# A fused attention kernel: queries, late weights and row sums reordered in its start

## The reference

```
# first block, per image (1024 pixels, 256 channels)
x_ln = layernorm(x);  q = x_ln @ wq + bq
o    = gelu(depthwise_conv7x7_stride2(q as an image) + dw_b)     # 16 x 16 positions
pos  = refs + tanh(o @ pw_w)                                     # 256 sampling points
samp = bilinear(x, pos)                                          # from x itself
k, v = samp @ wv + bv, then @ mk_w, @ mv_w;  qh = q @ mq_w
att  = softmax(qh kh^T) vh                                       # 8 heads, 1024 x 256
z    = att @ mo + mo_b + x;  y = gelu(layernorm(z) @ mlp_w + mlp_b) + z
# second block, per image
theta, phi, g = y @ w_theta, maxpool(y @ w_phi), maxpool(y @ w_g)
out  = y + sigma * (softmax(theta phi^T) g @ w_o + b_o)
```

## Time and profile before

| | us |
|---|---|
| three runs, median (lowest to highest) | 514.73 (513.17 to 515.65) |
| the profiled execution, its time | 512.36 |
| its span, first to last instruction | 510.6 |
| PE, DVE, ACT, POOL busy over the span | 454.9, 286.2, 211.6, 120.1 |
| mean granted clock of PE | 0.98 |

### The profile page before, as it was taken

How to read it: one execution, slowest core, us unless ns; L and a number is a source line. 1 busy time by engine, 2 the same in 40 slices (tenths; PEclk the granted TensorE clock), 3 DMA queues, 4 the chain that set the end, 5 groups by cost and what they waited for, 6 DMA issues and landing times.

```text
span 510.6 us, 9319 instructions
## 1 busy us (share of the span) xinstructions
PE 454.9 (89%) x3743; PEld 318.8 (62%) x3743; DVE 286.2 (56%) x609; ACT 211.6 (41%) x338; POOL 120.1 (24%) x163
## 2 busy tenths in 40 slices
PE   6788979988989999989899999989899897888956
PEld 5657756645567576656686666656767564665735
DVE  4518446846673367667754345567546647625433
ACT  1122212545346045655333336745173664662230
POOL 5420301167003001681002003761030030100000
PEclk9999989989999999999999999999999998999978
DMA  7298866581947930293157801472226200000202
GB/s 211 76 168 171 163 101 126 85 169 65 137 69 99 233 54 3 85 124 64 42 101 103 164 3 46 90 111 27 83 42 86 83 3 2 1 2 2 82 2 83
DMA packets 30489, 42.90 MB, mean 84 GB/s; under 512 B 6075, under 2 KB 21230, under 8 KB 30446
## 3 DMA queue, kind: packets, MB, share of 16 engines
q1 hardware_dynamic: 23598, 34.82, 37.4%
q0 software_dynamic: 3584, 4.50, 3.8%
q10 hardware_dynamic: 3264, 2.99, 2.9%
HBM read 16.16 MB, written 4.19 MB: 40 GB/s over the span
## 4 chain that ended last, share of the span: by engine, by line
PE 57%; DVE 13%; DMA 10%; POOL 7%; issue 5%; ACT 5%; SPq 1%; ACTq 0%; DVEq 0%; POOLq 0%
PE ps_d L759 8%; PE ps_d L884 5%; PE ps_d L861 5%; PE ps_d L961 5%; PE ps_d L747 4%; PE ps_s L808 4%; DMA xa<-in_x_dram 4%; PE ps_v L850 4%; DMA corners<-in_x_dram,row_of 3%; PE ps_v L844 3%; PE ps_t L827 3%; PE ps_d L779 3%; POOL samp L1937 3%; DVE mx L1613 3%; PE ps_d L903 2%
## 5 line engine op out<-in xcount | busy, mean ns | idle before, releaser
L1226 ACT ACTIVATE prob<-ps_t 128x1024 f32<-128x1024 f32 x64 | 65.4, 1021 | 95.8 <-PE ps_t L827 92.2
L1613 DVE TENSOR_REDUCE mx<-ps_s 128x4 f32<-128x1024 f32 x64 | 78.2, 1222 | 24.1 <-PE ps_s L808 23.2
L1909 POOL DMA_DIRECT2D q_st<-mx_t x64 | 34.0, 532 | 244.0 <-ACT mx_t L1218 226.0
L759 PE MATMUL ps_d<-cstack,conv_w 128*32 128x256 f32 x1024 | 59.0, 380 | 3.4 <-issue 1.8
L808 PE MATMUL ps_s<-k_st,q_st 96*128 96x256 f32 x256 | 49.9, 317 | 8.2 <-DVE mx L1613 7.1
L759 PEld LDWEIGHTS ps_d<-cstack,conv_w 128*32 128x32 f32 x1024 | 36.3, 108 | 23.9 <-issue 6.2
L808 PEld LDWEIGHTS ps_s<-k_st,q_st 96*128 96x128 f32 x256 | 35.9, 191 | 20.5 <-DVE mx L1613 12.6
L827 PE MATMUL ps_t<-q_st,k_st 98*128 98x256 f32 x256 | 42.6, 289 | 6.2 <-ACT zt L1285 3.0
L827 PEld LDWEIGHTS ps_t<-q_st,k_st 98*128 98x128 f32 x256 | 35.5, 192 | 8.9 <-issue 5.1
L1627 DVE TENSOR_TENSOR att<-ps_v,rden 128x256 f32<-128x256 f32 x32 | 13.6, 424 | 43.2 <-ACT rden L1237 43.2
L844 PE MATMUL ps_v<-prob,vh 128*32 128x256 f32 x512 | 35.1, 392 | 1.5 <-DVE att L1627 1.5
(11 more groups left out here) (178 smaller groups left out, 744.7 us busy)
## 6 DMA issues: line engine op xcount, KB each, us to landing
q_st<-q_parts SPq DMA_DIRECT2D x42, 256.0 KB, 5.6
xa<-in_x_dram SPq DMA_DIRECT2D x8, 512.0 KB, 9.6
z_all<-in_x_dram SPq DMA_DIRECT2D x8, 512.0 KB, 7.9
out_dram<-z_all SPq DMA_DIRECT2D x8, 512.0 KB, 2.6
cstack<-qpad SPq DMA_DIRECT2D x22, 180.5 KB, 5.7
k_st<-cstack SPq DMA_DIRECT2D x22, 128.0 KB, 4.2
q_st<-z_all SPq DMA_DIRECT2D x6, 256.0 KB, 5.7
cstack<-att SPq DMA_DIRECT2D x6, 180.5 KB, 9.8
```

What stands on the lines that cost most here:

```text
L759: ins = pe.matmul(ps[32 * k:32 * k + 32, 0, :], conv_w[:, cb * 4 + k, y, x, :], cstack[:, cb, k, y:y + HG_, x:x + WG_], start=n == 0, stop ...
L1226: drain(act.activation(prob[:, u % 2, 2 * pr:2 * pr + 2].rearrange("p h m s -> p (h m) s"), ps_t[:], ACT.Exp), t_ring, "t", b, u, pr)
L1613: drain(dve.tensor_reduce(mx[:, u % 2, half, :], ps_s[:], AX.X, ALU.max), s_ring, "s", b, u, half)
```

## The change

On PE, ACT and DVE the second query group of the first half goes ahead of the convolution, and both groups of the second half ahead of the keys; the opening order of the PSUM tiles is rewritten to match. The first half of image 1's convolution does 8, 3 and 2 steps (before 6, 4 and 3) in the ramp and in slots (0, 0) and (0, 1). The loads of for_rest are cut in two: three of them (for_output) are issued in slot (0, 3) behind z of image 0, eight (for_second) in slot (1, 0); PE and DVE wait for each where it is first used. On ACT row_deviation(0, [1]) stands ahead of the copy of the turned wq. On DVE two of the four statistics of the second half stand behind row_shift of the first, and query_lo(0, 1, [0]) ahead of the second sampled.

```diff
-STEPS_OF_1 = range(6), range(6, 10), range(10, 13), range(13, TAPS * TAPS)
+STEPS_OF_1 = range(8), range(8, 11), range(11, 13), range(13, TAPS * TAPS)
...
-    order += [("qh", 0, 0, 0)] + [("conv", 0, cb) for cb in range(CB)] + [("off", 0), ("qh", 0, 0, 1)]
-    order += [("qimg", 1, 1, jp) for jp in range(2)] + [("qimg", 1, 0, 0), ("qh", 0, 1, 0), ("kh", 0)]
-    order += [("qh", 0, 1, 1), ("qimg", 1, 0, 1), ("conv", 1, conv_halves(1)[0])]
+    order += [("qh", 0, 0, hg) for hg in range(NHG)] + [("conv", 0, cb) for cb in range(CB)] + [("off", 0)]
+    order += [("qimg", 1, 1, jp) for jp in range(2)] + [("qimg", 1, 0, 0), ("qh", 0, 1, 0), ("qh", 0, 1, 1)]
+    order += [("kh", 0), ("qimg", 1, 0, 1), ("conv", 1, conv_halves(1)[0])]
...
 # SP, slots
+                if b == 1 and s == 0:
+                    for_second.start(sp)
...
                     if s == 3:
                         behind_max_row(b, 3)
                         load_z(b)
+                        for_output.start(sp)
...
 # SP, ramp
             stack_conv(0, 1)
+
+
             load_a(1)
-            for_rest.start(sp)
             stack_q(0, 0, [0])
...
 # PE, slots
                     project(m, 1, 1)
+                    if m == 0:
+                        for_second.wait(pe)
                     project1(m, "tp", w_tp, 0)
...
                 if s == 7 and b == 0:
-                    for_rest.wait(pe)
+                    for_output.wait(pe)
...
 # PE, ramp
-            queries(0, 0, [0])
+            queries(0, 0)
...
             offsets(0)
-            queries(0, 0, [1])
             q_image(1, 1)
             q_image(1, 0, [0])
             setup_values()
-            queries(0, 1, [0])
+            queries(0, 1)
             pe.wait_ge(setup_act, A_ALL)
             keys(0)
-            queries(0, 1, [1])
...
 # ACT, ramp
                 setup_copy(t_wqt, ps_s[:, 0:2, :])
-                row_deviation(0, [1])
...
             row_deviation(0, [0])
+            row_deviation(0, [1])
             setup_queries()
...
-            query_hi(0, 0, [0])
+            query_hi(0, 0)
...
-            query_hi(0, 0, [1])
             setup_values()
-            query_hi(0, 1, [0])
+            query_hi(0, 1)
...
-            query_hi(0, 1, [1])
...
 # DVE, slots
+                    if m == 0:
+                        for_second.wait(dve)
                     g_projected(m)
...
-                    for_rest.wait(dve)
+                    for_output.wait(dve)
...
 # DVE, ramp
-            half_stats(0, second)
+            half_stats(0, second[:2])
             row_shift(0, first)
+            half_stats(0, second[2:])
...
-            query_lo(0, 0, [0])
+            query_lo(0, 0)
...
             positions(0)
-            query_lo(0, 0, [1])
...
             sampled(0, 0)
+            query_lo(0, 1, [0])
             sampled(0, 1)
-            query_lo(0, 1, [0])
+            query_lo(0, 1, [1])
...
-            query_lo(0, 1, [1])
```

More of the change, by code:

```diff
@@ L424, in wait @@
                 eng.wait_ge(self.sem, 16 * len(self.pairs))
-        for_q, for_norm, for_image, for_conv, for_taps, for_fused, for_keys, for_rest = [
-            Loads(f"loaded_for_{name}") for name in ("q", "norm", "image", "conv", "taps", "fused", "keys", "rest")]
+        for_q, for_norm, for_image, for_conv, for_taps, for_fused, for_keys, for_output, for_second = [
+            Loads(f"loaded_for_{name}") for name in ("q", "norm", "image", "conv", "taps", "fused", "keys", "output", "second")]
         for_q.add(consts[:], a["shape_constants"][:, 0:K_M32])
@@ L450, in build @@
         for_keys.add_to_all_rows(mvb_all[:], a["L0_conv_mv_b"])
-        for_rest.add_matrix(mo[:], a["L0_conv_mo_w"])
-        for_rest.add_to_all_rows(mob_all[:], a["L0_conv_mo_b"])
-        for_rest.add_matrix(mlp[:], a["L0_conv_mlp_w"])
+        for_output.add_matrix(mo[:], a["L0_conv_mo_w"])
+        for_output.add_to_all_rows(mob_all[:], a["L0_conv_mo_b"])
+        for_output.add_matrix(mlp[:], a["L0_conv_mlp_w"])
         for_image.add_to_all_rows(mlpb_all, a["L0_conv_mlp_b"])
         for row in range(3):
[L456 to L461, removed]
+            for_second.add_matrix(w_tp[:, :, row * C8:(row + 1) * C8], a["L1_conv_w_theta"])
+        for_second.add_matrix(w_tp[:, :, 3 * C8:4 * C8], a["L1_conv_w_phi"])
+        for_second.add_matrix(w_g[:], a["L1_conv_w_g"])
+        for_second.add(w_o[:], a["L1_conv_w_o"])
+        for_second.add_to_all_rows(bo_all[:], a["L1_conv_b_o"])
+        for_second.add(sigma[:], a["L1_conv_sigma"].rearrange("(a c) -> a c", a=1).broadcast_to([P, 1]))
         def qpad_tile(b, cb):
```

## The result

The changed kernel is slower. Over 21 runs of each its median is 518.12 us (514.59 to 523.11) against 515.65 (509.75 to 518.55); the ratio is 1.0058, 95% interval 1.0037 to 1.0078. So it lost about 3 us where 6.95 were forecast as a gain, and lies outside the range of 505.0 to 511.8. They serve for places and mechanisms, the ratios for sizes.

A forecast was written before the change was run, and what follows sets the result against it. PE was busy 89%, but idle waits in the ramp before image 0's first scores were taken as what the change could shorten. -6.85 - 0.4 + 0.3 = -6.95 us, against median 514.73 giving 507.8; range 505.0 to 511.8.

The forecast's parts named there:

- Front, -3.2 and start of the convolution at 28.6: Image 0's second half of normalised rows comes 3.2 us earlier; its convolution starts at 28.6 instead of 31.49, -2.9.
- DVE's rows of image 1 and PE's convolution both move by 2.9, so the gather's first issue is at 48.5: Ramp: rows of image 1 move with the planes, to 38; gather's first issue moves from 51.45 to 48.5.
- The gather lands earlier after its issue: Ramp: with three query part DMAs gone, last landing 6.6 to 13.1 us after first issue, formerly 13.1; middle taken, 58.4.
- rival A: Gather lands no sooner after its issue, 13.1 us again, because planes alone keep the engines full: 511.6 us, chance 0.15.
- Six query part DMAs took 13.06 to issue against a full queue: SP's queue in the ramp: hence three such DMAs beside the gather are worth 6.5 us at most, nothing at least.
- New wait of DVE, keys at clock 1.00, gap of 1.6: DVE's query_lo ends 59.3, after the gather's landing; keys start 61.4 (-5.25) and, after PE's 1.6 gap, take 1.1 less.
- First scores at most 6.6 after key_hi: Ramp's end: key_hi, key_lo and key DMAs take at most 6.6 us, so first scores at 70.1 at latest.
- Loads in slots, +0.3: Loads moved to slot 3 of image 0 and the slot after: max rows may be late; +0.3 us taken.
- rival C: Loads of slot 3 hold max rows near 117, costing 6.3 us, the later eight again: 520.1 at full, chance 0.03.
- What arrives earlier there shifts all of the rest: After the first scores nothing is tied to a clock time, so a gain there reaches the end.
- -6.85 at the first scores: End of the ramp: first scores at 69.6 instead of 76.45 us, the largest term of the sum.
- Rival B: Ramp: planes start earlier and overlap key weights by up to 2.5 us; planes 2 late: 509.8 us, chance 0.14.

The follow-up runs named there:

- the front alone: Kernel before with only row_deviation of the second half ahead of the copy and two of four statistics behind row_shift; 0.9889 of before (0.9823 to 0.9955).

## Why the prediction was wrong

- *Front, -3.2 and start of the convolution at 28.6*: right. PE's second products at 17.28 (17.2 forecast), convolution at 28.32, ratio of the front alone 0.9889.
- *"DVE's rows of image 1 and PE's convolution both move by 2.9, so the gather's first issue is at 48.5"*: **this step failed**. It counted PE's two halves as one block that shifts, and the rows of image 1 as moving with the planes, to 38. The rows' second half landed at 39.5 and the gather was issued at 55.94. In the two kernels in which all or the eight small loads stood ahead of the copies, with the new order, the first issue came at 48.83 and 48.97: the step is right where the copies are not in the way. The loads were costed for who waits for them and for what lies beside the gather, not for what they had kept apart: six copies came right behind the rows and under the fetch of PE's own program. The row that would have warned is the 1.76 us gap for "issue" ahead of the second half, with DMA full; the prediction neither priced nor named it. Its cost is 8.9 us at the first scores, against the kernel with all loads back.
- *The gather lands earlier after its issue*: right in the changed kernel, and for another reason. Its four indirect DMAs landed in 3.9 us at the median from their issue, the last 9.1 after the first issue, and DVE's second blend did not wait for them. But there the planes of image 1 were issued only at 60.22, behind all four, because PE had made the q images late. In the four kernels in which the query copies were issued by 43 and the planes went out 2.6 us after the gather's first issue, the last corners landed 10.6 to 12.1 after it, against 13.1 before. So planes alone keep most of the landing time, as rival A said: the copies' absence is worth 1.0 to 2.5 us and not the middle of the range (3.2). Beside copies the landing was as bad as before or worse (up to 15.8).
- *"Six query part DMAs took 13.06 to issue against a full queue"*: misread, and the upper end of 6.5 rests on it. The three copies of the first group took 2.97 and those of the second 1.85; between them SP waited 8.2 us for DVE to make the second group's parts (who waits, for whom: total us, times, longest):

```profile
SPq L571 <- DVE q_parts L1530: 8.2, 1, 8.2
```

- *New wait of DVE, keys at clock 1.00, gap of 1.6*: right (gap 1.83, keys 1.97), shifted by the step that failed. It holds only as long as the gather lands in time: the gap was 1.8 to 2.9 in eight of the kernels with the new order, and 5.1 and 6.6 in the two whose last corners came 14 us or more after the first issue.
- *First scores at most 6.6 after key_hi*: missed by about 1. It was 7.55 (72.73 to 80.28), and PE waited 2.2 to 2.3 for key parts in eight of the ten kernels with the new order. Why the key parts land later there was not tried.
- *Loads in slots, +0.3*: undersized in place. The wait that rival C described came, in the unit that it named, at 2.67 instead of its 6.3; with a clock fall behind it in this profile and in five others, and none in the other three with the three loads in slot 3. Rival C's mechanism is seen; it is not what made the kernel slower.
- *"What arrives earlier there shifts all of the rest"*: too simple. The lead of 2.9 us at the first scores that the new order has over the front alone shrank to 1.3 by the end, as other waits and clock falls filled in. Of the -6.85 at the first scores, the largest term of the sum, the part that the order was to give did not reach the median even where no block was held (0.9885 with it, 0.9886 without).
- Rival B (planes and key weights collide) did not occur. None of the rivals held the mechanism.

The Trainium skill's rule that each DMA engine takes turns between queues (DMA: Bandwidth & Descriptors, section Queues, rings and completion order) was read here for the gather alone. By it a block of 16 KB would wait for one turn of SP's queue. The measured time from the start of the second half to the packet went from 1.2 to 9 us with the number of copies, up to six, and no further with twelve; if that is a turn, it is a long one. The measurement decides; what bounds it stays open.

## What to carry to other kernels

Before a load is taken away from a busy stretch, ask what moves into its place, and include the engines' own instruction blocks among those who wait for the DMA engines. A gap with "issue" as its releaser while DMA is at full share is the sign of this. In this kernel large SBUF to SBUF copies should not be at the head of a queue when a long run of small matmuls is about to use up its block, nor right behind rows that an engine waits for. Moving work off a queue is worth only what the waiting engine then does earlier: split the change and time its parts, as here one part held the whole gain.

## What the runs showed of the hardware

PE consumed a 16 KB block in 7.2 us of convolution products. Its next block came 8.8 to 9.2 us after the second half had begun when six or twelve 256 KB copies within SBUF were queued by SP, but 1.2 to 3.3 us after with none to three. From six to twelve copies (one run) it did not grow. The block ahead of it came 6.2 to 6.6 us after the first half had begun in every kernel, beside planes and rows. With copies right behind them in the same queue the rows of image 1 landed 1 to 2 us later.

The granted clock also fell to half inside the second half of the convolution, right after the gap of 2.0 us ahead of it, in five kernels (window 38 to 42 of the front alone below, clock 0.57) and not in others with the same gap (1.00 in the kernel with all loads in the ramp). It makes the half last 9.0 to 9.3 us instead of 7.4 to 7.7. Those in which it fell include three of the four best (0.9878, 0.9886 and 0.9889), so a single profile does not tell how good a kernel is.

```profile
38.00:42.00 4.00, 4.00 (x51) 3.86 (x47) 3.93 (x18) 1.80 (x3) 0.00 (x0) 0.57 0.93 189
```
